# Output projection block by block, and behind the experts: residual, ratios and input weights loaded two tiles ahead, 24 buffers for the first batch's gathers

## The reference

```
y = y.reshape(b, l, d)
o = _layernorm(y, gamma, beta) @ Wo.T
x = x + o                                   # attention
hs = _L0_cond2_ref(x, ...)                  # sigmoid(x) * ratio
logits = hs_flat @ gate_weight.T            # 16 experts
...                                         # 6 experts of 16 are chosen for a token
for e in range(E):
    inter = jax.nn.silu(g) * u
    out = out + comb[:, e:e + 1] * (inter @ down_proj[e].T)
return y + shared_out
```

## Time and profile before

| | |
|---|---|
| median of three runs | 3676.23 us (3672.75 to 3680.26) |
| the profiled execution's own time | 3678.08 us |
| its span | 3676.3 us |
| PE busy | 3287.4 us, 89% |
| DVE busy | 2605.3 us, 71% |
| ACT busy | 1227.3 us, 33% |
| POOL busy | 511.8 us, 14% |
| granted clock of TensorE, mean | 0.948 of full speed |

### The profile page before, as it was taken

How to read it: one execution, slowest core, us unless ns; L and a number is a source line. 1 busy time by engine, 2 the same in 40 slices (tenths; PEclk the granted TensorE clock), 3 DMA queues, 4 the chain that set the end, 5 groups by cost and what they waited for, 6 DMA issues and landing times.

```text
span 3676.3 us, 37190 instructions
## 1 busy us (share of the span) xinstructions
PE 3287.4 (89%) x12621; PEld 2021.7 (55%) x12621; DVE 2605.3 (71%) x3645; ACT 1227.3 (33%) x2145; POOL 511.8 (14%) x404
## 2 busy tenths in 40 slices
PE   1979979979988999999999949899989999999999
PEld 1654654644645767777777714644464446444644
DVE  7888988889875677888888435664667456755664
ACT  2333343332422545434343223312341134113410
POOL 1003003003003111111111021120121012100200
PEclk9989989989999999999999978999999989999999
DMA  3212212212204778787878540223022311222011
GB/s 147 79 34 57 77 45 68 55 48 59 68 15 168 266 248 272 241 276 253 270 245 268 174 189 35 80 94 118 34 81 72 122 53 54 95 91 86 17 53 46
DMA packets 277070, 436.70 MB, mean 119 GB/s; under 512 B 52368, under 2 KB 189584, under 8 KB 264464
## 3 DMA queue, kind: packets, MB, share of 16 engines
q1 hardware_dynamic: 257200, 379.85, 30.9%
q0 software_dynamic: 19680, 54.46, 4.7%
HBM read 364.59 MB, written 93.77 MB: 125 GB/s over the span
## 4 chain that ended last, share of the span: by engine, by line
PE 62%; DVE 23%; DVEq 5%; ACT 5%; issue 2%; DMA 2%; POOL 1%; SPq 0%; ACTq 0%; POOLq 0%
PE bank L1029 13%; PE bank L1058 7%; PE bank L1302 6%; PE bank L1316 4%; PE bank L1324 4%; PE bank L1168 3%; PE bank L838 3%; PE bank L1229 3%; DVE sb_gla L1920 3%; PE bank L978 3%; PE bank L1035 2%; DVE sb_ratio L1878 1%; DVE sb_parts L1932 1%; DVE sb_ratio L1899 1%; PE bank L1024 1%
## 5 line engine op out<-in xcount | busy, mean ns | idle before, releaser
L1029 PE MATMUL bank<-sb_xT,sb_work 128*128 128x256 f32 x2304 | 513.2, 382 | 1.6 <-issue 0.8
L1029 PEld LDWEIGHTS bank<-sb_xT,sb_work 128*128 128x128 f32 x2304 | 439.3, 192 | 75.3 <-issue 17.5
L838 PE MATMUL bank<-sb_gla,sb_work 128*128 128x256 f32 x896 | 244.5, 423 | 64.7 <-DVE sb_work L1922 56.2
L1058 PE MATMUL bank<-sb_work,sb_hT 128*128 128x512 f32 (+1 forms) x666 | 296.1, 592 | 0.0
L838 PEld LDWEIGHTS bank<-sb_gla,sb_work 128*128 128x128 f32 x896 | 179.9, 208 | 123.5 <-DVE sb_work L1922 79.0
L1316 PE MATMUL bank<-sb_parts,sb_gla 128*128 128x512 f32 x512 | 238.5, 610 | 4.5 <-ACT sb_gla L1658 4.5
L1324 PE MATMUL bank<-sb_parts,sb_gla 128*128 128x512 f32 x512 | 230.8, 593 | 6.6 <-DVE sb_work L2510 6.6
L1168 PE MATMUL bank<-sb_parts,sb_hT 128*128 128x512 f32 x512 | 235.7, 621 | 0.0
L1716 POOL DMA_INDIRECT sb_parts<-scratch_h,sb_small x111 | 121.1, 1091 | 820.9 <-DMA sb_small<-scratch_ids 806.3
L1302 PE MATMUL bank<-sb_work,sb_parts 128*128 128x512 f32 (+2 forms) x640 | 227.5, 514 | 5.5 <-ACT sb_work L1671 5.5
L1058 PEld LDWEIGHTS bank<-sb_work,sb_hT 128*128 128x128 f32 (+1 forms) x666 | 121.8, 190 | 129.7 <-issue 129.6
(11 more groups left out here) (397 smaller groups left out, 5919.9 us busy)
## 6 DMA issues: line engine op xcount, KB each, us to landing
sb_work<-scratch_gu SPq DMA_DIRECT2D x63, 1408.0 KB, 7.1
sb_parts<-scratch_mx SPq DMA_DIRECT2D x16, 3072.0 KB, 11.3
sb_work<-moe_w SPq DMA_DIRECT2D x63, 512.0 KB, 6.6
scratch_y<-sb_work SPq DMA_DIRECT2D x48, 512.0 KB, 7.4
sb_parts<-scratch_fq SPq DMA_DIRECT2D x24, 1024.0 KB, 8.6
sb_work<-w_qkvg SPq DMA_DIRECT2D x64, 256.0 KB, 3.2
scratch_gu<-moe_w SPq DMA_DIRECT2D x32, 512.0 KB, 6.1
sb_parts<-fT SPq DMA_DIRECT2D x48, 256.0 KB, 5.7
```

What stands on the lines that cost most here:

```text
L838: mm = pe.matmul(dst.rearrange("p (h n l) -> p h n l", h=HPC, l=size), kS[u % 2][:, k * P:(k + 1) * P], late[:, :, k, :, 1, :], start=True ...
L1029: mm = pe.matmul(dst, egu[j % 3][:, which * NC + k, m * P:(m + 1) * P], xt[j % 2][:, k, :], start=(k == 0), stop=(k == NC - 1))
L1058: mm = pe.matmul(bank(YB[s]), einter[j % 2][0:n, a:a + P], edn[j % 3][0:n, m * D:(m + 1) * D], start=(m == 0), stop=(m == EC - 1))
```

## The change

- `PIECES` becomes (3, 0, 1, 2): the query is projected second, the key third; POOL's `qa` waits for the second evacuation instead of the third.
- The output projection runs with the output block outside and the input chunk inside; the matmuls for the variance stand behind the first block. The banks are used in the order 7, 1, 2, 3.
- h1 stands in the memory of `ysq` (in the last batch in R[0]), and its four chunks are announced one by one; DVE multiplies chunk c - 1 with the ratio right behind the residual add of block c. The logits are computed chunk by chunk.
- Pieces 24 and 25 move from ahead of the output blocks to behind h1; 26 and 27 move from there to the first step of the shared expert, behind `picks`; 28 and 29 to the second step.
- While tile 61 of the experts is up (`j == NTL - 2`), SP waits for the older stores and issues the loads of residual, both ratios and three of four input weights (1 MB each). The fourth and `wm6` follow behind the last store, and `wout` waits for the end of `weigh`.
- The first batch's 24 gathers have a buffer each and wait for nothing; they share six semaphores, four on each, and `weigh` waits for four at a time.

```diff
-        PIECES = (3, 1, 0, 2)
-        OB = (1, 2, 3, 7)
+        PIECES = (3, 0, 1, 2)
+        OB = (7, 1, 2, 3)
         yT = w(8192, NC * T)
-        h1 = yT
         ysq = w(10240, NC * T)
+        H1 = [ysq] * (NB - 1) + [R[0]]
...
-        SHARED_PIECES = (range(29, 30), range(30, 34), range(34, 36), range(36, 40), range(40, 44), range(44, 48))
+        SHARED_PIECES = (range(26, 28), range(28, 34), range(34, 36), range(36, 40), range(40, 44), range(44, 48))
...
+                if j == NTL - 2:
+                    for i in range(2):
+                        sp.wait_ge(st_r[i].sem, 32 * (NB * NC // 2))
+                        sp.wait_ge(prep_st[i].sem, 16 * (NPREP // 2))
+                    sp.wait_ge(st_x1.sem, st_x1.at(NB - 1, 1))
+                    load_batch(0)
+                    load_r3(0)
+                    for m in (2, 3, 1):
+                        sp.dma_start(wzx[:, m, :, :], scratch_fq[m]).then_inc(ld_sw.sem, 16)
...
             for b in range(NB):
-                for m in (2, 0, 1, 3):
+                for m in (2, 0, 1, 3) if b else (0,):
...
+                if b == 0:
+                    sp.wait_ge(y_sum.sem, y_sum.at(0, NT))
                 for m in range(2):
                     sp.dma_start(wout[:, m, :, :], scratch_fq[4 + m]).then_inc(ld_so.sem, 16)
...
-                for k in range(NC):
-                    pe.wait_ge(ln_cent.sem, ln_cent.at(b, k + 1))
-                    for oc in range(NC):
+                for oc in range(NC):
+                    for k in range(NC):
+                        if oc == 0:
+                            pe.wait_ge(ln_cent.sem, ln_cent.at(b, k + 1))
                         mm = pe.matmul(bank(OB[oc]), wo[:, k, oc * P:(oc + 1) * P], ch(yT, k),
                                        start=(k == 0), stop=(k == NC - 1))
-                        if k == NC - 1:
-                            mm.then_inc(o_done.sem, 1)
-                    if k == 0:
+                    mm.then_inc(o_done.sem, 1)
+                    if oc == 0:
...
-                pe.wait_ge(h1_ready.sem, h1_ready.at(b, 1))
-                for t in range(NT):
-                    for k in range(NC):
+                h1 = H1[b]
+                for k in range(NC):
+                    pe.wait_ge(h1_ready[k].sem, h1_ready[k].at(b, 1))
+                    for t in range(NT):
                         mm = pe.matmul(bank(7)[:, t * NE:(t + 1) * NE], ch(h1, k)[:, t * P:(t + 1) * P],
-                                       gwT[:, k * NE:(k + 1) * NE], start=(k == 0), stop=(k == NC - 1))
+                                       gwT[:, k * NE:(k + 1) * NE], start=(k == 0 and t == 0),
+                                       stop=(k == NC - 1 and t == NT - 1))
...
                 for u in range(b * NC, (b + 1) * NC):
-                    pool.wait_ge(g_evac.sem, g_evac.at(u, 3))
+                    pool.wait_ge(g_evac.sem, g_evac.at(u, 2))
                     if u:
                         pool.wait_ge(g_qe.sem, g_qe.at(u - 1, 1))
                     pool.tensor_tensor(qa, qS[u % 2], aS[u % 2], ALU.mult).then_inc(g_pool.sem, 1)
+                    pool.wait_ge(g_evac.sem, g_evac.at(u, 3))
...
-                    if k >= NYG:
+                    if b:
                         pool.wait_ge(y_acc.sem, k - NYG + 1)
-                    pool.indirect_dma_start(yg[k % NYG], None, d_y,
+                    pool.indirect_dma_start(yg[k % NYG] if b else yg0[k], None, d_y,
                                             bass.IndirectOffsetOnAxis(ap=physu[:, k:k + 1], axis=0))\
-                        .then_inc(y_rows[k % NYG].sem, 16)
+                        .then_inc(y_rows[k % NYG if b else k // 4].sem, 16)
...
-                if b + 1 < NB:
-                    for n in (24, 25):
-                        ratio_piece(r0 + n)
+                def gate1(c):
+                    dve.wait_ge(sig1.sem, sig1.at(b, c + 1))
+                    tt(ch(H1[b], c), ch(H1[b], c), ch(R[1], c), ALU.mult).then_inc(h1_ready[c].sem, 1)
+
                 x = X1[b % 2]
                 for oc in range(NC):
...
                     stt(out=ch(x, oc), in0=ch(ysq, oc), scalar=wob[:, oc:oc + 1], in1=ch(x, oc),
                         op0=ALU.add, op1=ALU.add).then_inc(x1a.sem, 1)
-                dve.drain()
-                for c in range(NC):
-                    dve.wait_ge(sig1.sem, sig1.at(b, c + 1))
-                    q = tt(ch(h1, c), ch(h1, c), ch(R[1], c), ALU.mult)
-                q.then_inc(h1_ready.sem, 1)
+                    if oc:
+                        gate1(oc - 1)
+                gate1(NC - 1)
+                dve.drain()
                 if b + 1 < NB:
-                    for n in (26, 27, 28):
+                    for n in (24, 25):
                         ratio_piece(r0 + n)
...
                     if j == 0:
+                        picks(b)
                         if not last:
-                            ratio_piece(6 * (2 * NC * b + NC) + SHARED_PIECES[0][0])
-                        picks(b)
+                            for n in SHARED_PIECES[0]:
+                                ratio_piece(6 * (2 * NC * b + NC) + n)
...
+                    if b:
+                        dve.wait_ge(y_rows[n % NYG].sem, 16 * (n // NYG + 1))
+                    else:
+                        dve.wait_ge(y_rows[n // 4].sem, 16 * 4)
+                    src = yg[n % NYG] if b else yg0[n]
```

26 lines of the change are left out of this document (10 added, 16 removed).

## The result

| | before | after |
|---|---|---|
| median (lowest to highest) | 3674.49 us (3672.13 to 3680.26) | 3632.36 us (3625.82 to 3637.57) |
| span of the profiled execution | 3676.3 us | 3626.6 us |
| granted clock, mean | 0.948 | 0.960 |

The ratio is 0.9884, 95% interval 0.9872 to 0.9897: 42 us faster, where 28 were forecast (between the two spans it is 49.7). The two later sets of the same kernel gave 0.9906 and 0.9919, 34 and 30 us. In the trace after, a line of the first part stands 7 to 10 lines lower than in before (L937 is L944, L952 L959, L978 L986, L1987 L1997), in the third part L1112 is L1120, L1128 L1136, L1168 L1176 and L1726 L1735.

A forecast was written before the change was run, and what follows sets the result against it. DVE was taken to bound batches 1 to 3, PE the last batch's projection and logits, gathers the tail. Gains 15.9 + 8.0 + 0 + 4 = 27.9 us gave 3649 us, range 3641 to 3661.

The forecast's parts named there:

- Output projection, batches 1 to 3: Output projection through shared expert: DVE sets the batch's end, and removing its idle time gains 5.3 us a batch, 15.9 us.
- DVE's three waits: Shared expert, batches 1 to 3: DVE's waits for PE of 1.68, 3.04 and 1.56 us would go.
- the 5.8 us by which the first scores lie ahead of DVE's first level: Next batch's start: slack of 5.8 us that would hide some 2 us of PE matmuls at half clock.
- I take the full level, since no stop is left: Router's logits, batches 1 to 3: TensorE at full clock, 3.73 us for 32 records instead of 7.01.
- Last batch: Last batch's projection and logits: PE's time counts in full, logits end 8.0 us earlier (8.9 at full clock, 5.9 at half).
- Order of the weight pieces: Attention units, query projected second and POOL's product earlier: taken as 0 us, with bounds -6.6 and +1.15.
- Loads two tiles ahead: Layer 1's loads during the last expert tiles: covered by expert matmuls, cost nothing, no gain booked.
- 24 buffers: Gathers between experts and layer 1: POOL issues without waiting for DVE, 4 us gained, bounds 1 and 7.5.
- the case of larger gains: Whole kernel: a time of 3640 us or less, beyond all the stated bounds; chance 0.04.
- the choked gathers: Gathers before layer 1: issue held until an earlier one lands, 4.95 us each, 3729 us; chance 0.03 with any other loss.
- The one on a low clock at the logits: Router's logits: TensorE's clock stays low, gain only 20.7 us, time 3656 us; chance 0.22.
- The rule of the Trainium skill: Gathers beside DVE's sums: a gather held for a whole 0.75 us sum, layer 1 starting 4 us later than before.

The follow-up runs named there:

- rival T of the tail's run: Kernel before with only layer 1's loads two tiles ahead and 24 gather buffers, guessed to give 13 us, all from this edit; measured 3665.41 us, 0.9977.

## Why the prediction was wrong, point by point

- **Output projection, batches 1 to 3: right in mechanism, a little too large.** The logits wait 0.5 us and run at the full level in the first two batches, the router starts 7.7, 7.7 and 7.3 us earlier counted from the projection (7.8 forecast), DVE's three waits are gone, and a batch is 5.4, 4.8 and 4.9 us shorter from its projection to the next first level (forecast 5.3). What was too sure is the cover: "the 5.8 us by which the first scores lie ahead of DVE's first level". The scores hang on POOL's drain, and that on the landing of 24 scatters; in four of seven traces with the new projection and the old place of the memset DVE waited 1.9 to 6.6 us there. The part alone gave 19 us instead of 23.9. "I take the full level, since no stop is left" was too sure as well: in the ten traces with the new projection the logits keep the full level in 10 of 40 batches, and in the others the mean granted clock over them is 0.71 to 0.95. In batches 1 to 3 this costs nothing, for the router waits for piece 25 (25.5 to 25.9 us behind the projection's start, whatever the logits take).
- **Last batch: right in size.** 7.5 us from the projection's start to the logits' end (8.0 forecast), and 7.5 to 8.8 over the ten traces, as the clock holds or not.
- **Order of the weight pieces: the step "I take 0" was too low.** The bounds held +1.15, for the first scores alone. The trace means over 17 executions say 2.8 us in the first batch and 0.4 in each later one; alone it gave 4 us, with an interval that holds 0.
- **Loads two tiles ahead: this is the step that failed.** "Nobody waits for these loads: cost nothing" is right for the cost, but the sum put their worth at nothing too, without a reason; it is the largest error of mechanism. I had seen 1.02 and 424 GB/s and drew no time from it. The loads alone gave 12 us (0.9967, 7 to 17 by the interval), and 8.9 us between first gather and layer 1 in the trace.
- **24 buffers: the 4 us were booked to the wrong edit.** Alone they lose 1.9 us between the gathers and layer 1, and with the loads ahead 3.3 (in the changed kernel): I had priced the three more sums rightly (6.7 us instead of 4.17) but had read the 2 us gaps between gathers as POOL waiting for DVE, when DVE was waiting for rows. The sum, 42.8 us, fell near the forecast 44.7 since the errors have opposite signs: luck in the number, not a right mechanism.
- **Layer 1's first batch, 7.9 us: not forecast, and only in part to be put down to the change, if at all.** The same stop of 1.44 us (L1148 before, L1156 after) leads to another clock:

```profile
2172.45:2186.45 14.00, 14.00 (x26) 4.77 (x27) 0.00 (x0) 0.43 (x1) 0.00 (x0) 0.80 0.00 0
...
2216.45:2258.45 42.00, 39.88 (x96) 17.91 (x95) 18.19 (x25) 8.53 (x15) 0.00 (x0) 0.84 0.00 0
```

(before) and after

```profile
2134.00:2148.00 14.00, 13.93 (x29) 4.96 (x30) 0.91 (x3) 1.57 (x4) 0.00 (x0) 0.88 0.24 100
...
2178.00:2212.00 34.00, 33.15 (x94) 15.27 (x94) 17.10 (x23) 7.78 (x13) 0.00 (x0) 1.00 0.00 0
```

  In the 17 traces the stage from L1128 to L1240 takes 77.95 to 78.9 us where the first 14 us had a mean granted clock of 0.83 or more (11 traces, the query's order alone among them), and 81.1 to 86.0 where it was 0.78 to 0.81 (6 traces, one with the loads ahead). The forecast started from the trace of before that had it worst. Chance alone is not shown either: with the loads ahead the stage is short in 9 of 10 traces (mean 78.7 us), without them in 2 of 7 (mean 82.1 us). So 3 to 4 us of it may belong to the loads, as rival T of the tail's run had it for all of it; why the clock rises earlier or later was only seen, not shown.
- **The whole.** Parts: 19 + 4 + 8.5 = 31.6 us; the changed kernel's three sets: 42, 34 and 30. Against the forecast's terms the projection is 4.8 us less, the query's order 4.0 more and the tail 4.5 more, together 3.7. Each part is uncertain by 4 to 6 us, so they neither show nor exclude that the parts help each other by a few us. The rest up to 42 is most likely where one set of a kernel happens to fall (16 executions of the changed kernel on at least two chips run from 3625.8 to 3644.3, median 3637). By the two later sets the time would be 3642 and 3646, inside the range of 3641 to 3661: that the first set lies 9 us below the range is partly bad luck; that the loads' 12 us were missing from the forecast, which hid behind the 4 us booked to the buffers, is not.
- **Slips of the sum.** The written time is 0.7 us above its own sum: 3676.23 less 27.9 is 3648.3, not 3649, and the rivals' times are up to 1.2 us high in the same way. The chance of "faster", 0.93, leaves out the case of larger gains, 0.04.
- **The rivals.** Of them, the choked gathers can be put aside (1.25 to 1.71 us between issues with 24 buffers, one gap of 2.3). The one on a low clock at the logits held in part: for the second half in two of the four batches here, and in most batches of the other traces, yet without its price in batches 1 to 3. The rule of the Trainium skill ("SBUF — State Buffer", Who interferes with whom), by which a gather could be held for a whole sum, would have made the step 2.0 us. The trace shows no such hold in the mean step, 1.41 us; single steps up to 1.71 us would fit a wait for the rest of a running sum, which no run here tells apart.

## What to carry to other kernels

Where urgent transfers and patient ones start together, the share column (1.02) is a time to be priced: move the patient ones to either side, and count buffers only afterwards. Behind many small scatters, a drain or a wait for a store's landing can be a bound of 5 to 20 us, as measured here; keep those, and what is queued behind them, out of the way before a gain upstream uses up their cover. Before a difference of a stage is put down to an edit, the stage should be read in a second trace of the same kernel.

## What the hardware showed that was not expected

- With a drain of POOL behind 24 indirect transfers the next product started only 10.7 to 20.2 us behind the last issue's end, although its inputs were there, in 28 of 42 seams (14 traces, three each; in the other 14 its input came last). With the drain ahead of them it was 2.7 to 6.0 us (3 traces), as soon as the input came.
- The same 1 MB store took 4.9 to 15.6 us to land in the seams. In one window there the transfer engines were busy for 0.89 of the time at 11 GB/s, 87.1% by SP's own packets and 1.0% by the scatters'.
- One stop of 1.44 us left TensorE's clock at the full level in 11 traces. In 6 the clock fell afterwards, in four of them 1.2 to 1.4 us behind the stop's end and in two 11 us behind it. In the 11 the clock had risen 3.0 to 4.8 us behind the first matmul of layer 1, in the 6 only 5.3 to 6.1 us behind it, some 40 us before the stop; why this goes together is not shown.
